# Attention and mixture of experts on one core: the residual travels with the sorted rows, and the experts' scatters write

## The reference

```python
xn = layernorm(x)
x = x + attn(xn) + ffn(xn)
# attn: gated linear attention, 4 heads, chunks of 64 in the reference
#   o = chunk_gla(q, k, v, log_sigmoid(xn @ Wgk + bgk) / 16)
#   o = o * rsqrt(mean(o * o) + eps) * gnorm_w * silu(xn @ Wg)
#   return o @ Wo
# ffn: each token goes to the one expert of eight with the largest router logit
#   h = gelu(xn @ w1[e] + b1[e]);  y = h @ w2[e] + b2[e]
#   out = softmax_weight_of_e * y
```

## Time and profile before

| | us |
|---|---|
| median of 3 runs (389.52 to 390.5) | 389.59 |
| the profiled execution | 389.28 |
| its span, from the first to the last instruction | 387.5 |
| PE busy in the span | 373.4 |
| DVE busy | 314.5 |
| ACT busy | 291.8 |
| POOL busy | 279.1 |
| 71 scatters at L619 on POOL, busy | 112.9 |
| 64 placings at L577 on POOL, busy | 64.9 |

### The profile page before, as it was taken

One profiled execution on the slowest core, in us unless ns is written; L12 is line 12 of the kernel. 1 busy time (PEld: TensorE's weight loads), 2 busy tenths in 40 slices (PEclk: granted clock), 3 DMA queues, 4 the chain that ended last, 5 costly groups with the idle time before them and its releaser, 6 DMA issues.

```text
span 387.5 us, 13901 instructions
## 1 busy us (share of the span) xinstructions
PE 373.4 (96%) x3963; PEld 321.2 (83%) x3963; DVE 314.5 (81%) x859; ACT 291.8 (75%) x889; POOL 279.1 (72%) x245
## 2 busy tenths in 40 slices
PE   7999999999999999999999999899999999999992
PEld 7667777777777877787777877899999999999991
DVE  5988999989898988888888878777788787777761
ACT  4889987788888888888888886566666667666661
POOL 8003534878787888888788873288888888888886
PEclk9999999999999999999999999999999999999997
DMA  8946788456555445575654423155555455556440
GB/s 231 257 140 198 223 270 292 134 170 191 170 184 161 138 147 157 158 200 162 191 157 150 131 79 81 54 67 72 64 72 70 65 70 71 69 71 76 75 37 6
DMA packets 59106, 51.45 MB, mean 133 GB/s; under 512 B 7200, under 2 KB 51392, under 8 KB 59072
## 3 DMA queue, kind: packets, MB, share of 16 engines
q1 hardware_dynamic: 45936, 42.07, 38.8%
q0 software_dynamic: 12272, 8.54, 15.3%
q10 hardware_dynamic: 864, 0.40, 0.4%
HBM read 33.14 MB, written 18.30 MB: 133 GB/s over the span
## 4 chain that ended last, share of the span: by engine, by line
PE 83%; DVE 4%; DMA 3%; issue 3%; ACT 2%; POOL 2%; SPq 2%; DVEq 0%; ACTq 0%; POOLq 0%
PE psA L988 16%; PE psVG L976 15%; PE psVG L771 11%; PE psT L867 8%; PE psO L825 7%; PE psQK L757 5%; PE psT L851 4%; PE psVG L790 4%; PE psO L839 3%; PE psKS L814 3%; POOL out_dram L619 2%; SPq L355 2%; DMA x_all<-in_L_attn_x_dram 1%; ACT E L1160 1%; DMA gcB<-decay_rows 1%
## 5 line engine op out<-in xcount | busy, mean ns | idle before, releaser
L619 POOL DMA_INDIRECT out_dram<-yw,sidx x71 | 112.9, 1590 | 28.8 <-DVE sidx L1700 17.5
L1160 ACT ACTIVATE E<-gcB,ngc 128x128 f32<-128x128 f32 x256 | 78.3, 395 | 0.7 <-DMA gcB<-decay_rows 0.7
L577 POOL DMA_INDIRECT sorted_rows<-x_all,pos_i x64 | 64.9, 1015 | 13.4 <-issue 12.8
L561 POOL TENSOR_TENSOR rms<-msn,neg_half 128x8 f32<-128x8 f32 x32 | 54.4, 1699 | 26.5 <-DVE msn L1492 22.5
L554 POOL TENSOR_SCALAR_AFFINE_SELECT E<-E 128x1024 f32<-128x1024 f32 x32 | 35.2, 1099 | 36.5 <-ACT E L1160 24.9
L1142 ACT ACTIVATE th<-psVG,x_all 128x256 f32<-128x256 f32 x64 | 26.9, 470 | 20.4 <-issue 11.6
L988 PE MATMUL psA<-xT_all,v_sb 128*128 x288 | 38.3, 276 | 1.0 <-issue 0.6
L976 PE MATMUL psVG<-xgT,gcB 128*128 128x128 f32 x288 | 37.9, 275 | 0.0
L988 PE MATMUL psA<-xT_all,th 128*128 x280 | 37.4, 276 | 0.0
L976 PE MATMUL psVG<-xgT,E 128*128 128x128 f32 x280 | 37.0, 275 | 0.0
L867 PE MATMUL psT<-wo_sb,oT 128*128 128x128 f32 x256 | 36.9, 287 | 0.0
(11 more groups left out here) (214 smaller groups left out, 950.6 us busy)
## 6 DMA issues: line engine op xcount, KB each, us to landing
gcB<-decay_rows SPq DMA_DIRECT2D x32, 512.0 KB
sorted_rows<-blank SPq DMA_DIRECT2D x12, 396.0 KB, 5.0
xg<-sorted_rows SPq DMA_DIRECT2D x71, 66.0 KB
x_all<-in_L_attn_x_dram SPq DMA_DIRECT2D x16, 256.0 KB, 5.2
out_dram<-res SPq DMA_DIRECT2D x32, 128.0 KB
eqB<-decay_exp_rows SPq DMA_DIRECT2D x32, 64.0 KB
w1b<-in_L_ffn_w_dram SPq DMA_DIRECT2D x8, 256.0 KB
xT_all<-in_L_ffn_w_dram SPq DMA_DIRECT2D x32, 64.0 KB
```

Of the source, the lines that this page charges most:

```text
L561: nc.gpsimd.tensor_tensor(rms[j][:], msn[j][:], neg_half[:, 0:2 * H], ALU.pow).then_inc(rms_ready, 1)
L577: nc.gpsimd.indirect_dma_start(out=sorted_dram, out_offset=bass.IndirectOffsetOnAxis(ap=pos_i[:, t:t + 1], axis=0), in_=x_all[:, t, :], in ...
L619: nc.gpsimd.indirect_dma_start(out=out_rows, out_offset=bass.IndirectOffsetOnAxis(ap=sidx[j][:], axis=0), in_=yw[j][:], in_offset=None, bo ...
L1160: last = nc.scalar.activation(E[j][:, k, h * P:(h + 1) * P], gcB[j][:, k * H + h, :], ACT.Exp, bias=ngcf[:, bass.ds((s * 2 + k) * H + h, 1)])
```

## The change

The residual no longer goes to the output tensor. `x_all` gets 128 columns more per tile, which first hold the transposed rows (`xT_all` becomes a view of them), later the residual, and for the first 32 tiles in the end w2. The sorted table's rows become 260 values (1040 bytes) instead of 132. A tile is placed when its residual is there, as whole rows, for the tiles 0 to 53. Tiles 54 to 63 are placed in two halves of 130 values: the first (raw row, 1/std, -mean/std) on the old schedule, the second (weight, token number, residual) when its residual is ready, by ten further indirect DMAs in steps 30 to 32 and behind them. The first eight blocks are loaded in halves too; the second halves wait for all ten. `weigh` is split: `take` adds the bias straight out of PE's result, and the weighing, which now also adds the residual, comes one block later; in the first turn it waits for the second halves, from behind block 4 on. The scatter writes instead of adding. The larger table takes 24 clears of about the old size each; the first five stand ahead of `store_decays(0)`. SP's stores of `res` are dropped. w2 is loaded from step 20 instead of 18, after the first 32 tiles have been placed.

```diff
-    CLEARS = 12
+    XR = XW + D
+    XH = XR // 2
+    CLEARS = 24
...
+        x_all = sb("x_all", [P, TILES, XR])
+        xT_all = x_all[:, :, XW:XR]
+        w2_sb = xT_all[:, 0:EXP * FC, :].rearrange("p (e c) d -> p e c d", c=FC)
...
+            sp.wait_ge(blank_made, 2)
+            for k in range(5):
+                clear(k)
+
             gc_rows = gc_dram.rearrange("(a p) t -> p a t", p=P)
...
-                if inside(i, j, -3, SEQS):
-                    store_res(*turn(i, j, -3, 2))
...
             step(0, 0)
-            clear(0)
-            clear(1)
+            for k in range(5, 8):
+                clear(k)
...
+            sp.wait_ge(placed_low, EXP * FC * 16)
+            with sp.Fori(W2_FROM, W2_FROM + EXP // 2) as i:
...
             def load_block(i, j):
                 b = i * R + j
-                if not (isinstance(i, int) and i == 0):
-
-                    sp.wait_ge(dve_y, (b - R + 1) * Y_N)
+                sp.wait_ge(y_out, b - R + 1)
                 sp.dma_start(xg[j][:], sorted_dram[bass.ds(b * P, P), :]).then_inc(xg_loaded[j], 16)
...
+            sp.wait_ge(placed, (TILES - EXP * FC) * 16)
             for j in range(R):
-                load_block(0, j)
+                sp.dma_start(xg[j][:, 0:XH], sorted_dram[j * P:(j + 1) * P, 0:XH]).then_inc(xg_loaded[j], 16)
+            sp.wait_ge(res_placed, (TILES - WHOLE) * 16)
+            for j in range(R):
+                sp.dma_start(xg[j][:, XH:XR], sorted_dram[j * P:(j + 1) * P, XH:XR]).then_inc(xr_loaded, 16)
...
+            def place_res(t):
+                pool.wait_ge(res_ready, t // 2 + 1)
+                nc.gpsimd.indirect_dma_start(out=half_rows, out_offset=bass.IndirectOffsetOnAxis(ap=half_i[:, 1, t - WHOLE:t - WHOLE + 1], axis=0),
+                                             in_=x_all[:, t, XH:XR], in_offset=None).then_inc(res_placed, 16)
...
+                if s * 2 - 6 >= WHOLE:
+                    place_res(s * 2 - 6)
+                    place_res(s * 2 - 5)
...
+            for t in range(SEQS * 2 - 4, TILES):
+                place_res(t)
...
-                                             in_=yw[j][:], in_offset=None, bounds_check=TOKENS - 1, oob_is_err=False,
-                                             compute_op=ALU.add).then_inc(scattered[j], 16)
+                                             in_=yw[j][:], in_offset=None, bounds_check=TOKENS - 1, oob_is_err=False).then_inc(scattered[j], 16)
...
+            def take(i, j):
+                b = i * R + j
+                dve.wait_ge(y_ready, b + 1)
+                if not (isinstance(i, int) and i == 0):
+                    dve.wait_ge(y_out, b - R + 1)
+                nc.vector.tensor_tensor(yb[j], psY[j % 2][:, 0:D], wbuf[j % 4][:, FF + FC:WB], ALU.add).then_inc(y_taken, 1)
+
             def weigh(i, j):
                 b = i * R + j
-                c_y.begin(b)
+                if isinstance(i, int) and i == 0:
+                    dve.wait_ge(xr_loaded, R * 16)
...
+                nc.vector.tensor_copy(sidx[j][:], xg[j][:, D + 3:D + 4]).then_inc(sidx_ready, 1)
+                dve.wait_ge(y_taken, b + 1)
+                nc.vector.scalar_tensor_tensor(yw[j][:], yb[j], xg[j][:, D + 2:D + 3], xg[j][:, XW:XR], ALU.mult, ALU.add).then_inc(y_out, 1)
...
-            weigh(0, 0)
+            take(0, 0)
             residual(last, 1)
-            e = block_step(0, 1, e)
-            for j in range(2, R):
+            done = 0
+            for j in range(1, R):
                 e = block_step(0, j, e)
+                while done < WEIGHED_BY[j]:
+                    weigh(0, done)
+                    done += 1
...
+            weigh(TURNS - 1, TAIL - 1)
...
+WHOLE = 54
+W2_FROM = 10
+WEIGHED_BY = [0, 0, 0, 0, 1, 3, 5, 7]
```

More of the change, by code:

```diff
@@ L219, in build_layer @@
         oT = sb("oT", [P, 4, P])
-        res = [sb(f"res{j}", [P, 2, D]) for j in range(2)]
         sidx = [sb(f"sidx{j}", [P, 1], I32) for j in range(R)]
-        xg = [sb(f"xg{j}", [P, XW]) for j in range(R)]
+        xg = [sb(f"xg{j}", [P, XR]) for j in range(R)]
         xgn = [sb(f"xgn{j}", [P, D]) for j in range(4)]
@@ L229, in build_layer @@
         hid = [t[:].rearrange("p k (c n) -> p (k c) n", n=P) for t in (v_sb[0], th)]
-        yb = [sb(f"yb{j}", [P, D]) for j in range(2)]
+        yb = [pr[:].rearrange("p r n -> p (r n)")[:, j * D:(j + 1) * D] for j in range(R)]
         yw = [sb(f"yw{j}", [P, D]) for j in range(R)]
@@ L415, in step @@
                     load_gc(i + 1, j)
-            sp.wait_ge(blank_made, 2)
             step(0, 0)
-            clear(0)
-            clear(1)
+            for k in range(5, 8):
+                clear(k)
             step(0, 1)
             store_decays(1)
-            clear(2)
-            clear(3)
+            for k in range(8, 11):
+                clear(k)
             step(1, 0)
-            sp.dma_start(w1b[:, :, FF + FC:WB], b2.partition_broadcast(P)).then_inc(w_loaded, 16)
+            for k in range(11, 15):
+                clear(k)
             step(1, 1)
@@ L429, in _ @@
             sp.wait_ge(eq_stored[1], 16)
[L430 to L433, removed]
+            for k in range(15, 19):
+                clear(k)
+            step(2, 0)
+            for k in range(19, CLEARS):
+                clear(k)
+            step(2, 1)
+            sp.dma_start(w1b[:, :, FF + FC:WB], b2.partition_broadcast(P)).then_inc(w_loaded, 16)
             with sp.Fori(3, 3 + EXP // 2) as i:
@@ L598, in step @@
                 if n:
-                    place_rows(t)
+                    place_rows(tiles[0])
                 if n == 3:
-                    place_rows(t + 1)
+                    place_rows(tiles[1])
                 if s + 1 < SEQS:
@@ L673, in logits @@
                     g = S * GT + q
-                    last = nc.tensor.matmul(ps_lgT[S][q * LS:(q + 1) * LS, :], wr_pad[:], xT_flat[:, g * GT * P:(g + 1) * GT * P],
+                    last = nc.tensor.matmul(ps_lgT[S][q * LS:(q + 1) * LS, :].rearrange("p (k n) -> p k n", n=P), wr_pad[:], xT_all[:, g * GT:(g + 1) * GT, :],
                                             start=True, stop=True)
@@ L1462, in slots_to_positions, with half_positions @@
                 late(nc.vector.tensor_copy(pos_i[:], pos[:]))
+            def half_positions():
+                for a in range(2):
+                    late(nc.vector.tensor_scalar(half_f[:, a, :], pos[:, WHOLE:TILES], 2.0, float(a), ALU.mult, ALU.add))
+                late(nc.vector.tensor_copy(half_i[:], half_f[:]))
             def scale_wo():
@@ L1664, in _ @@
             step(3, 1, aside=block_experts)
-            step(4, 0)
+            step(4, 0, behind=half_positions)
             step(4, 1)
@@ L1713, in block_step @@
                     e = expert_of(*turn(i, j, 4, R))
-                weigh(i, j)
+                take(i, j)
+                if not (isinstance(i, int) and i == 0):
+                    weigh(*turn(i, j, -1, R))
                 return e
@@ L1769, in placed_by, with placed_in @@
     return n
+def placed_in(s):
+    whole, part = 0, WHOLE
+    for k in range(PLACE_FROM, s + 1):
+        tiles = []
+        for _ in range(placed_by(k) - placed_by(k - 1)):
+            if whole < min(WHOLE, (k - 2) * 2):
+                tiles.append(whole)
+                whole += 1
+            else:
+                tiles.append(part)
+                part += 1
+    return tiles if s >= PLACE_FROM else []
 ROUTE = {"az0": 4, "g0": 5, "gdiff0": 7, "az1": 15, "g1": 16, "onehot": 21, "gdiff1": 23, "count": 24, "nb": 27, "all": 29}
```

102 lines of the change are left out of this document (42 added, 60 removed).

## The result

The changed kernel takes **418.44 us** (median of 4 runs, 416.68 to 418.94) against 389.55 (389.22 to 390.50) on the same chip: a ratio of 1.073, 95% interval 1.069 to 1.077. It is slower, as forecast, but by 28.9 us and not by 10.8; the range ended at 406.5. The profiled execution has a span of 416.3 us.

The account below looks back on a forecast made before the run. PE, busy 96% of the span, was taken to set the pace. Terms -2.2 + 3.5 + 1.2 + 4.9 + 1.5 + 1.9 = +10.8 on 389.28 gave 400.1 us, range 390.5 to 406.5.

Parts of the forecast that it names:

- Scatters write instead of adding: Expert stage: without the add a scatter takes 1.0 us instead of 1.56, so POOL no longer runs behind PE.
- The rival of the slow POOL: Expert stage: the bound, not the add, costs the 0.58 us, scatters keep their old pace; 404.4 us, chance 0.13.
- the faster rival: Expert stage: scatters had been pacing PE, which without them runs freer; 386.3 us, chance 0.12.
- The front: Near the start: decay rows queue behind five clears, ACT's exponentials start late; +3.5 us, between 0 and 6.
- half clock: Behind PE's new gaps in the front and at block 8, work may run at half clock; +1.9 us in all.
- The rival of the decay rows slipping past the clears: Near the start: the decay rows do not queue, the front's 3.5 us go; 396.6 us, chance 0.10.
- The halves on POOL: End of attention: added indirect DMAs push back the last rms and PE's transposition that needs it; +1.2 us.
- Blocks 8 and 9: Expert stage: PE waits for reloads of xg held up by weighing that needs the second halves; +4.9 and +1.5 us.
- The rival of the halves landing in time: Block 8: the eight loads land by 256.9, leaving 0.9 us instead of 4.9; 396.1 us, chance 0.07.
- my four terms: First rms to last bias add: last rms 1.2, block 8 4.9, block 9 1.5, clock 1.9; together +9.5 us.
- taken at nothing: Further clears, half tables and copies, wider rows, placings' waits on residuals, w2's wait, dropped stores: each taken as costing nothing.
- The end: Behind the last bias add: the last scatters finish sooner, 4.7 us instead of 6.9; -2.2 us.

Follow-up runs that it names:

- e3: The changed kernel with scatters that add again instead of writing: 408.04 us.
- e2: The kernel before with scatters that write instead of adding, nothing else changed: 400.92 us, ratio 1.030.
- e9: e2 with a memset of 0.58 us on POOL behind each writing scatter: 389.37 us, ratio 1.001.
- e10: e2 with each scatter also waiting for PE's first layer of three blocks later: 388.15 us, ratio 0.996.
- e1: The changed kernel with its first five clears moved behind the first loads of the decay rows: median 409.29 us, runs from 402.08 to 410.95.
- e7: The kernel before with five of its twelve clears put ahead of the store of the decay rows: 395.47 us, ratio 1.016.
- e4: The changed kernel without residual halves: all tiles placed whole without waiting for the residual, which goes to an unread tile: 409.42 us.
- e14: e1 with a memset of 0.3 us on POOL behind each half placing and each scatter: 403.49 us.
- e18: e1 with scatters that add again, so neither the front's clears nor writing scatters: 401.38 us, ratio 1.032.
- e13: e4 with the five clears behind the first decay loads and a 0.3 us memset on POOL behind each scatter: 394.61 us, ratio 1.014.
- e12: e1 with each scatter also waiting for PE's first layer of three blocks later: 404.62 us.
- e5: e2 with PE's expert stage as a loop of four blocks instead of written out: 404.04 us.
- e11: e2 with half rows, 128 pieces of 256 bytes instead of 512: 401.46 us.
- e17: e2 with every index moved beyond the bound, so that no row is written: 399.86 us, ratio 1.027.
- e8: The kernel before with PE's expert stage as a loop of four blocks, nothing else changed: 396.56 us.

## Why the prediction was right in sign and wrong in size

**The step that failed** is "Scatters write instead of adding": "That is 1.3 us per block against PE's 1.9, so POOL no longer runs behind." As far as it goes this came true. By line (ns least, median, most; first and last start) the scatter of after answers L619 in the earlier trace rows:

```profile
L632 POOL DMA_INDIRECT out_dram<-yw,sidx x71: 978/980/1247, 272.4 to 413.6; - x71
```

The rival of the slow POOL is out: with the bound and without the add the scatter costs what a placing does, so the 0.58 us were the add's. But I took a POOL that is no longer slow to be free of effect on PE and looked only for waits and buffers. The adds, 1.86 us from start to start, had kept POOL from bunching; the writes can follow each other in 1.28. Whenever two or three become ready together (the backlog behind block 8, or blocks that come close behind a stall), PE's signals are late, and PE then waits for ACT. Each delay makes the next blocks bunch, which fits the recurrence every 6 us: three blocks. It is 13.4 us in after (e3 against after) and 15.1 in e2, and near 1 with the writes spaced (e9, e10). It is the greater part of the 18 us that I missed: 13.4, 4.4 more in the front than forecast and 0.7 less gained at the end, against 0.5 less in the rest of the middle.

That fast and slow scatters stand on the same PE pace was also what I used against the faster rival, and there it held: with writes spaced PE's middle is 342, not less than 341.

**The front: right mechanism, mis-sized term.** "So the decay rows land near 25.5 ... the exponentials start near 29.6" became 27.96 and 32.08. The store was issued later, at 21.57 and not 19.84, behind 4.57 us of SP issuing the clears, and its DMA took 6.37 us, against 5.5 expected. The exponentials' 6.0 us are the far end of my 0 to 6. Another 1.9 us came behind it: PE ran at half clock after its wait. I had put half clock at one block's 1.9 us for the whole kernel. Windows (stretch; busy us of PE, PEld, DVE, ACT, POOL; granted clock; DMA share; GB/s) of the front and of the stretch behind the freeze at 261 us:

```profile
36.00:40.00 4.00, 4.00 (x21) 3.65 (x20) 3.83 (x11) 3.66 (x10) 0.72 (x2) 0.50 0.98 325
264.00:268.00 4.00, 2.82 (x16) 2.82 (x17) 1.05 (x3) 2.54 (x10) 0.00 (x0) 0.75 0.35 83
```

The rival of the decay rows slipping past the clears is out: e1 and e7 show them queued.

**The halves on POOL: right.** Two stand between the last two rms and push the last one from 2.45 us behind its predecessor to 4.56:

```profile
249.40 2.04 POOL L558 TENSOR_TENSOR rms<-msn,neg_half 128x8 f32<-128x8 f32 x1 [1.89 <-DVE msn L1503]
251.63 1.04 POOL L585 DMA_INDIRECT sorted_rows<-x_all,half_i  x1 [0.19 <-issue]
252.97 0.96 POOL L585 DMA_INDIRECT sorted_rows<-x_all,half_i  x1 [0.30 <-issue]
253.96 1.67 POOL L558 TENSOR_TENSOR rms<-msn,neg_half 128x8 f32<-128x8 f32 x1
```

**Blocks 8 and 9: right in sum, not in form.** I expected gaps of 4.9 and 1.5 us. DVE does wait for the reloads, at the places named, but PE's wait there is short, since the freeze in the half placings had already cost it 3.16 us at 265:

```profile
273.91 0.35 DVE L1701 TENSOR_SCALAR xgn<-xg 128x128 f32<-128x128 f32 x1 [1.99 <-DMA xg<-sorted_rows]
...
277.98 0.34 DVE L1701 TENSOR_SCALAR xgn<-xg 128x128 f32<-128x128 f32 x1 [2.08 <-DMA xg<-sorted_rows]
```

```profile
265.18 1.34 PE L984 MATMUL psVG<-xgT,gcB 128*128 128x128 f32 x8 [3.16 <-ACT xgT L1286]
...
274.31 0.33 PE L975 MATMUL psQK<-ident,xgn 128*128 128x128 f32 x1 [0.66 <-DVE xgn L1701]
...
278.38 0.33 PE L975 MATMUL psKS<-ident,xgn 128*128 128x128 f32 x1 [1.80 <-DVE xgn L1701]
```

3.16 + 0.66 + 1.80 = 5.6 against 6.4. That the sum comes out is partly luck, since the freeze is no step of the forecast. Without the half placings (e4, PE's timeline) the reloads alone make gaps of 0.59 and 1.43 us, against 0.9 and 1.5 forecast:

```profile
264.84 0.33 PE L958 MATMUL psQK<-ident,xgn 128*128 128x128 f32 x1 [0.59 <-DVE xgn L1679]
...
268.53 0.33 PE L958 MATMUL psKS<-ident,xgn 128*128 128x128 f32 x1 [1.43 <-DVE xgn L1679]
```

With the halves and without their freeze the wait shows whole, 6.4 us at block 8 alone in e14, where the spacing also ends the halves some 2 us later. The rival of the halves landing in time is out: SP issues their loads in after from 265.12 on. The load of block 8 was issued at 271.70 and DVE used it 2.2 us later; I had taken 2.3. The Trainium skill, page "DMA: Bandwidth & Descriptors", section "Anatomy of one DMA — SWDGE (gpsimd) path", fits a DMA of GpSimd's queue by 2.0 us plus bytes over 436 GB/s, and the 2.3 was an estimate by that formula. This trace agrees with it, with 2.2 us, for one load on SP's queue.

Without front and writing scatters the middle is 8.9 us longer in e18 and 9.0 in e3 (350.2 and 350.3), against the 9.5 of my four terms. Single terms are not separated by that, and some of it lies where the forecast put nothing: in after, block 0's transposition, ahead of the last rms, is 2.1 us later than in before, counted from the first rms (1.2 in e18, 0.7 in e13). So something that I had taken at nothing (wider rows, more clears, the placings' waits) was not; which of them, stays open.

**The end: nearly right.** -1.5 instead of -2.2. The last bias add starts at 410.88 and the last scatter 2.75 us later, not 2.15: POOL starts 0.86 us behind a row set that is ready, where I had put 0.1.

```profile
410.88 0.29 DVE L1708 TENSOR_TENSOR pr<-psA,E 128x128 f32<-128x128 f32 x1 [0.98 <-PE psA L996]
...
413.63 0.98 POOL L632 DMA_INDIRECT out_dram<-yw,sidx  x1 [0.30 <-issue]
```

## What to carry to other kernels

Making an engine off the critical path faster also changes when it acts: before speeding up POOL's indirect DMAs, ask what had spaced them, and keep them spaced (a wait on an event of the pacing engine cost nothing in e10, but could not space a backlog in e12). A transfer put ahead of a small one that an engine stands waiting for cost its whole length here (2.0 MB, 6 us), and then half clock besides (1.9 us). Cut the span at rows that all variants share, the end of the front and the last result of the pacing engine: the two errors here would have been mixed up in the total.

## What the runs showed of the hardware that I had not expected

In the expert stage POOL's indirect DMAs, issued 1.3 to 1.5 us from start to start, delay what PE tells ACT and DVE (or PE's work itself): a copy of ACT that otherwise starts 0.3 to 0.5 us behind PE's transposition starts 0.6 to 0.9 us behind it for two in a row, and up to 5.0 us for longer rows (e4), even if no row is written (e17). Some 1.9 us apart they do not (e9, e10). The delay needs neither PE's instruction fetches (e5) nor the bytes (e11, e17). By what path POOL's issuing holds up PE's signals the runs don't show. The Trainium skill, page "Trainium Architecture — The Big Picture", section "What this means for kernel authors", calls the engines independent but for semaphores and names the port pair of DVE and GpSimd as the only contention among engines at the on-chip buffer; this trace shows a dependence of PE's signals on POOL besides. In the expert stage of the kernel before nothing of the kind is seen, as its adds leave 1.86 us between starts. Its placings do start in pairs 1.35 us apart during the attention (as at 75.27 and 76.62), and PE has no gap of 0.2 us or more there from 100 to 231 us; whether a signal is late in the slack of the other engines the rows do not show.

A loop instead of written-out blocks on PE made the kernel before 7.3 us slower over 16 turns (e8), some 0.46 us a turn, where I had expected 0 to 0.3.
